# Order of EM sums and updates against the output matmuls and output updates, in a conv and clustering kernel

## What is computed

```python
for _ in range(EM_ITERS):                                  # 10
    diff2 = ((data[:, :, None, :] - mu[:, None, :, :]) ** 2 / var[:, None, :, :]).sum(-1)
    logp = -0.5 * (diff2 + logdet[:, None, :] + k * log2pi) + jnp.log(wts)[:, None, :]
    resp = jax.nn.softmax(logp, axis=2)
    Nk = resp.sum(1)
    mu = jnp.einsum('bpn,bpk->bnk', resp, data) / Nk[..., None]
    ex2 = jnp.einsum('bpn,bpk->bnk', resp, data ** 2) / Nk[..., None]
    var = jnp.maximum(ex2 - mu ** 2 + EPS, EPS)
    wts = Nk / P
```

## Time and profile before

| | |
|---|---|
| median of 3 runs | 2816.44 us |
| the profiled execution, its own time | 2820.66 us |
| its span | 2818.9 us |
| busy PE, DVE, ACT, POOL | 78%, 57%, 46%, 30% |
| chain that ended last, by engine | PE 43%, DVE 24%, issue 13%, DMA 8%, DVEq 7% |
| DMA | 808 MB, 287 GB/s on average |

### The profile page before, as it was taken

One profiled execution on the slowest core, in us unless ns is written; L12 is line 12 of the kernel. 1 busy time (PEld: TensorE's weight loads), 2 busy tenths in 40 slices (PEclk: granted clock), 3 DMA queues, 4 the chain that ended last, 5 costly groups with the idle time before them and its releaser, 6 DMA issues.

```text
span 2818.9 us, 35575 instructions
## 1 busy us (share of the span) xinstructions
PE 2187.6 (78%) x9881; PEld 1308.5 (46%) x9881; DVE 1599.9 (57%) x2832; ACT 1308.4 (46%) x1710; POOL 847.9 (30%) x1481
## 2 busy tenths in 40 slices
PE   8986779877997779877997789777987787445544
PEld 3366324434554345444653446443644455334433
DVE  0063461577547762677457762777357754887343
ACT  5530243545555455454554554545455454333333
POOL 0000121343333422333234332333233423444332
PEclk9985798888898888988898888888898888677777
DMA  6620144987889878987889787887798887667898
GB/s 256 261 97 0 75 174 169 340 306 308 319 333 343 323 304 320 345 309 307 335 328 351 293 326 315 340 322 303 314 354 318 328 324 279 255 244 280 315 327 329
DMA packets 109825, 808.07 MB, mean 287 GB/s; under 512 B 10880, under 2 KB 10880, under 8 KB 11392
## 3 DMA queue, kind: packets, MB, share of 16 engines
q1 hardware_dynamic: 109696, 806.58, 74.6%
HBM read 538.10 MB, written 268.44 MB: 286 GB/s over the span
## 4 chain that ended last, share of the span: by engine, by line
PE 43%; DVE 24%; issue 13%; DMA 8%; DVEq 7%; POOLq 2%; POOL 1%; ACT 1%; SPq 1%; ACTq 0%
PE ps L811 18%; PE ps L629 17%; DMA out<-xres 7%; DVE xres L1162 7%; DVE logp L1036 4%; DVE prod L838 4%; PE ps L640 4%; DVEq L1166 3%; DVE part L851 3%; DVE prod L1048 3%; DVEq L1050 2%; DVE odds L851 2%; PE ps L796 1%; PE ps L772 1%; PE ps L745 1%
## 5 line engine op out<-in xcount | busy, mean ns | idle before, releaser
L629 PE MATMUL ps<-xin,taps 128*64 128x512 f32 (+1 forms) x4608 | 1083.0, 624 | 12.0 <-DMA xin<-x 11.4
L1162 DVE SCALAR_TENSOR_TENSOR xres<-ps,scale,xres 128x1024 f32<-128x1024 f32 (+2 forms) x768 | 675.0, 924 | 469.2 <-PE ps L811 323.2
L811 PE MATMUL ps<-interp,pairs 128*128 128x256 f32 (+1 forms) x2304 | 694.7, 474 | 198.5 <-DVE xres L1162 106.9
L811 PEld LDWEIGHTS ps<-interp,pairs 128*128 128x128 f32 x2304 | 568.4, 262 | 313.1 <-issue 198.4
L478 POOL TENSOR_TENSOR interp<-cst 128x2048 f32<-128x2048 f32 x128 | 476.1, 3719 | 657.9 <-PE ps L811 639.9
L629 PEld LDWEIGHTS ps<-xin,taps 128*64 128x64 f32 x4608 | 339.5, 137 | 669.3 <-issue 667.0
L568 ACT ACTIVATE xres<-xres,shift 128x2048 f32<-128x2048 f32 x256 | 499.9, 1993 | 146.0 <-DMA xres<-x 145.8
L573 ACT ACTIVATE junk<-xin 128x2048 bf16<-128x2048 f32 x256 | 487.5, 1904 | 25.9 <-issue 18.3
L796 PE MATMUL ps<-part,ones 128*128 128x34 f32 x160 | 46.6, 384 | 336.5 <-DVEq L852 336.5
L557 ACT ACTIVATE resp<-logp 128x32 f32<-128x32 f32 x160 | 27.9, 221 | 593.4 <-DVEq L1038 593.4
L431 POOL TENSOR_TENSOR coef<-mu,ivar 128x16 f32<-128x16 f32 x80 | 17.6, 220 | 702.4 <-DVEq L856 702.4
(11 more groups left out here) (166 smaller groups left out, 1383.1 us busy)
## 6 DMA issues: line engine op xcount, KB each, us to landing
xin<-x SPq DMA_DIRECT2D x128, 2048.0 KB, 7.9
xres<-x SPq DMA_DIRECT2D x256, 1024.0 KB, 6.0
out<-xres SPq DMA_DIRECT2D x256, 1024.0 KB, 6.5
cst<-consts SPq DMA_DIRECT2D x1, 400.0 KB, 3.0
wg<-w_guide SPq DMA_DIRECT2D x1, 256.0 KB, 12.5
wgx<-w_guide_x SPq DMA_DIRECT2D x1, 256.0 KB, 11.1
wf<-w_fuse SPq DMA_DIRECT2D x1, 256.0 KB, 11.1
wd<-w_down SPq DMA_DIRECT2D x1, 18.0 KB, 2.9
```

Of the source, the lines that this page charges most:

```text
L629: mm = pe.matmul(half[:, :, 1:] if kx == 0 else half, taps[:, 2 * t + i, n, :], tap_input(h, i, ky, kx), start=n == 0, stop=n == len(TAPS) ...
L811: mm = pe.matmul(ps[:, PS_UP + pos // 4, (pos % 4) * W:(pos % 4 + n) * W], pairs[:, m, :], interp[:, pos:pos + n, :].rearrange("c r w -> c ...
L1162: m = dve.scalar_tensor_tensor(dst, up[:, pos * W:(pos + r1 - r0) * W], sc, dst, ALU.mult, ALU.add)
```

## The change

On PE, `mixture_sums` comes behind the output matmuls in every stage that makes output, not only in stage 8. On DVE, `after_taps` comes behind the output update in iterate steps of stages that make output (2 to 8). Its other phases keep their place. All waits and all operations stay as they are; only their order on these two engines changes.

```diff
--- before.py
+++ after.py
@@ -797,7 +797,7 @@
                                   part[:, :, :].rearrange("c n k -> c (n k)"),
                                   start=True, stop=True).then_inc(em_sum, 1)
 
-                    if phase == "iterate" and do_conv:
+                    if phase == "iterate" and not do_out:
                         mixture_sums()
                     if do_out:
                         pe.wait_ge(interp_ready, o + 1)
@@ -813,7 +813,7 @@
                                                interp[:, pos:pos + n, :].rearrange("c r w -> c (r w)"),
                                                start=True, stop=True)
                             mm.then_inc(up_ps[half], 1)
-                    if phase == "iterate" and not do_conv:
+                    if phase == "iterate" and do_out:
                         mixture_sums()
 
                 def round_(t, u, phase, em):
@@ -1146,7 +1146,7 @@
                     o = g - 2 * STEPS
                     if do_em:
                         before_taps(j - 1, 1 - p, u, h, phase, em)
-                    if do_em:
+                    if do_em and not (do_out and phase == "iterate"):
                         after_taps(j - 1, 1 - p, u, h, phase, em)
                     if do_out:
                         for i in range(2):
@@ -1164,6 +1164,8 @@
                                 if i == 1:
                                     m.then_inc(up_taken[half], 1)
                             dve.drain().then_inc(result[i], 1)
+                    if do_em and do_out and phase == "iterate":
+                        after_taps(j - 1, 1 - p, u, h, phase, em)
 
                 def round_(t, u, phase, em):
                     for h in range(2):
```

## The result

The changed kernel takes 2859.4 us (median of 4 runs, 2849.5 to 2866.3) against 2815.7 us of the kernel before (4 runs, 2810.7 to 2822.4) on the same chip: ratio 1.0151, 95% interval 1.0111 to 1.0191, some 43 us slower. The profiled execution has a span of 2853.5 us (2818.9 before), so the traces have to explain 35 us; the other 8 or 9 us between the medians are in no trace. Stages 0 and 1 run until the first output matmul of stage 2, at 499.7 us before and 497.3 after (the EM iterations of stage 1 run from 319 to 427 us; the times said above for stages 0 and 1 are too late, and the earlier trace rows, at 325 us, do lie in stage 1).

The account below looks back on a forecast made before the run. Bound by expectation, output matmul and output update following one another. Stages 2 to 7 give -28 us, stage 8 +33, sum +5: 2826 against the profiled 2820.66, forecast as 2822 since that execution is 4.2 above the median; range 2798 to 2868.

Parts of the forecast that it names:

- rival 1: Iterate steps: interp gets in before L1037 and holds it, period 20.8 us in stages 2 to 7; 2860 us, 22%.
- The bare chain: EM update, POOL coefficients, lconst and interp with nothing covering them: 10.08 us, period 20.35 instead of 20.45 in stages 2 to 7.
- What ends the output update: Stages 2 to 7: PE's second half of the output matmuls decides, so DVE's output update is done at E+10.27.
- E: The end of POOL's interp op in an iterate step, from which the prediction counts times in us.
- First iterate step: Stages 2 to 7: its coefficients come from the start phase, so the next output matmul comes 4.3 us earlier.
- Stage 8: Same chain without convolution: 20.7 instead of 16.67 us, +32 in eight steps; first step +5.6, last some -5; +33 in all.
- Which op gets in first: DVE's two logp ops behind lconst: both slip in ahead of POOL's interp, which starts 0.18 to 0.29 us behind lconst.
- the forecast case: Both logp ops ahead of interp: -28 us in stages 2 to 7, +33 in stage 8; 2822 us, 53%.
- The case given 15%: Iterate steps: interp gets in before L1037 in about half the steps only; 2841 us, 15%.
- What a held op costs: With L1037 held by interp: period 20.8 us, +2.8 per stage, and +3.3 at the last step, where transposes wait.
- The rule on the port pair: SBUF port shared by DVE and POOL: first issuer blocks the other; read strictly, waiting interp would go before L1037.
- Rivals 2 and 3: Stages 2 to 7: PE fast, DVE not held, 2719 us, 5%; last stage loses little, 2789 us, 5%.

Follow-up runs that it names:

- pe_order_only: The kernel before with only PE's new order (sums matmul behind the output matmuls), DVE's order as before: 2709.6 us, ratio 0.9619.
- dve_order_only: The kernel before with only DVE's new order (EM update behind the output update), PE's order as before: 3114.1 us, ratio 1.1058.
- the gap drained: The changed kernel with two memsets, each with a drain, on POOL between lconst and interp in tile 1's iterate steps: 2819.9 us, ratio 1.0009.
- gap_and_stage8: The changed kernel with two drained memsets before interp in tile 1's iterate steps, and DVE's old order in stage 8: 2794.8 us, ratio 0.9929.
- pe_order_interp_first: The kernel before with PE's new order, DVE's old one, and POOL's interp moved ahead of the EM coefficients: 2725.9 us, ratio 0.9668.

## Why the prediction was right, and where it was not

The forecast was 2822 with 2798 to 2868, most of the chance on slower; 2859 lies inside, and 2860 was the time given to rival 1. That the median falls on 2860 is in part luck: rival 1 took the logp op as held in all ten steps, and it is held in four. By the prediction's own prices, four held steps with the tenth among them give -4.3 - 0.5 + 1.05 + 3.3 (five periods at -0.1, three at +0.35), or -0.45, per stage and some 2847 in all (an estimate). The rest is a term that was sized too low, of which more below, and the 8 to 9 us between the medians that are in no trace. Point by point:

- **Output matmuls leave the wait for part.** Right. They start 0.05 us behind interp's end (0.34 in the forecast), and PE's half alone is worth 106 us (pe_order_only).
- **The bare chain.** Right: 20.42 us measured in the steps without a held logp op (20.30 in stage 3), 20.35 worked out; 20.75 in stage 8 for 20.7; 25.5 for 25.4 in dve_order_only by the same terms.
- **What ends the output update.** Right in time, wrong in path. The forecast had DVE done by E+10.0 and PE's second half deciding at E+10.27. In the trace the update starts at E+4.98, behind part, takes 5.32 us without a wait for PE, and ends at E+10.30: DVE decides. That the two times agree is luck.
- **First iterate step.** Right: the second output matmul comes 33.6 us behind the last start step instead of 38.0, -4.4 for -4.3. Over six stages the mean is -4.8.
- **Stage 8.** Right: +32.5 in the trace for +33 (5.9, 32.7 and -6.0 for 5.6, 32 and -5); 25 and 42 by the medians of two pairs of runs.
- **Which op gets in first.** This is the step that failed in the forecast case: "I take it that both logp ops slip in ahead". They do in five of the six steps of tile 0 (in the first one interp comes long before both, as it did before, and holds L1036 for 2.65 us). They do not in the four of tile 1, without exception in seven stages. There POOL issues interp 0.18 us behind lconst instead of 0.29; in 3 of the 28 steps it is 0.37, but L1037 is later by as much, and interp is 0.05 ahead of it all the same. The case given 15%, "in about half the steps", is what happened. That interp's start varies was read from the rows of before, but taken for scatter: it goes by tile, in the trace of before too. In POOL's stream tile 0's iterate steps are the body of a loop with u in a register and the four of tile 1 are written out in line; that this makes the difference of 0.11 us was not tried.
- **What a held op costs.** The size was off, and this is why the time is that of rival 1 while only four steps in ten are held. Its period was right (20.92 for 20.8, 20.85 in stage 3). The step behind the tenth was not: +3.3 was worked out for the wait of the transposes, measured is +5.5. The wait is there (3.61 us), and behind it PE is at the 1.2 GHz level (granted clock 0.50), and transposes take 0.9 and taps 0.9 us more. With the gap drained the step takes 19.6 us, where the forecast case said 19.65.
- **The sum.** By the trace -4.8 + 0.8 + 5.4 = +1.4 per stage, six stages +9, where -28 was forecast. The step behind the tenth is 5.1 us longer than with the gap drained (24.68 and 19.55, means of six). 3.6 of that are the wait; the other 1.5, some 9 us in six stages, go with the low clock (an estimate; no run kept the wait and raised the clock). The other steps of these stages and stage 9, for which nothing was forecast, give -8.0 and +3.6. gap_and_stage8 shows the forecast case for these stages as a kernel of its own: -24 us (-26 to -14 by its interval) for -28.
- **The rule on the port pair.** The Trainium skill, "SBUF — State Buffer", "Who interferes with whom", states that whoever issues first holds the shared port pair for the whole instruction. For interp the rows agree at a resolution of 0.1 us: with interp issued 0.05 or 0.03 us ahead of L1037 it is DVE that waits for 3.6 us, with interp 0.06 behind it is not. L1036 being in progress at that time gives DVE no claim for the next op. The other half is not shown for the logp ops: interp takes 3.61 us where it starts 0.14 us before L1036 ends, and 3.65 where it starts with L1037 just begun, so neither holds it by more than 0.04. Read strictly, the rule was the better guide than the overlap of the two logp ops, by which I had decided.
- **Faster, and little loss in stage 8.** Rivals 2 and 3 fell: esum is held 3.07 us in the 35 steps in which neither logp op is, and stage 8 lost its 32 us.

What stays open: why the other steps of stages 2 to 7 scatter between 525 and 542 us among the kernels (528.7 in the changed one, 541.5 in gap_and_stage8). Transfers have 0.9 of the time in the iterate steps of the faster kernels, so part of what is gained there may be given back in the steps behind; no run took a transfer away.

## What to carry to other kernels

When an order of work on one engine is turned so that a wait goes, write down what was running under the moved piece: here 1.7 us of EM update had a chain of 8 us of another engine behind it, hidden by the 5.4 us update that it was moved past. Try each half of such a change alone, since one was worth -3.8% and the other took it back. Where GpSimd has one long op and VectorE many short ones, place the long op beside VectorE work that it does not hold (here the update that reads PSUM, and the reduce of part: 1.28 and 1.29 us in every trace), and look at which short ops in the trace are longer than their shortest.

## What the runs showed of the hardware that was not expected

- A difference of 0.1 us in the issue of one op decides 3.4 us, the same way every time: in seven stages of the changed kernel the same four iterate steps are held (28 of 70), and two memsets with drains in these steps are worth 40 us by the medians.
- Transposes run at the pace of the granted clock: eight take 1.04 us directly behind output matmuls and 1.92 us where PE has waited 3.6 us and the row shows 0.50.
- Small ops are held as long as large ones: the 128x16 op mu2 of 0.18 us takes up to 3.08 us in pe_order_interp_first.
